# Which engine copies the attention output out of PSUM, and when in a head's turn

## The chip, the cores and the metric

The kernel runs on one core of one Trainium2 chip. The metric is the device time of one execution in microseconds (us). The kernel before was run three times: median 3234.82 us, lowest 3233.41, highest 3235.3.

## What is computed

A residual stream of 4 sequences of 1024 tokens with 128 channels goes through eight blocks: linear attention, a mixture of experts, full attention, the same mixture of experts, causal attention, a one-expert mixture, a row-sum attention, and the one-expert mixture again. Only the third block bears on the change. Cut to what matters:

```python
def _L0_attn_b_ref(hidden_states, Wq, bq, Wk, bk, Wv, bv, Wo, bo):   # 16 heads of 8
    q = (hidden_states @ Wq.T + bq).reshape(b, s, HEADS, HEAD_DIM) * SCALE
    k = (hidden_states @ Wk.T + bk).reshape(b, s, HEADS, HEAD_DIM)
    v = (hidden_states @ Wv.T + bv).reshape(b, s, HEADS, HEAD_DIM)
    scores = jnp.einsum('bqhd,bkhd->bhqk', q, k)
    probs = jax.nn.softmax(scores, axis=-1)
    out = jnp.einsum('bhqk,bkhd->bqhd', probs, v).reshape(b, s, d)
    return out @ Wo.T + bo
```

With 4 sequences and 16 heads there are 64 heads (the code's HEADS), each with 1024 queries and 1024 keys.

## The kernel before, in words

`full_attention` (L1956) first projects queries, keys and values (`project_qkv`) and writes them to DRAM, then runs `attend` (L1041), and last `attention_output` (L1727), which reads what `attend` stored. Each engine has its own program; programs are joined by counting semaphores, which the code wraps as "steps" (`o_read.wait(pe, n)` waits until step n of `o_read` is done). Every engine carries out its own instructions in order.

`attend` is written as turns: `run` (L1087) calls each engine's `step(i, n)` for n from 0 to 66. Turn n works on up to four heads at once. Head i = n has its **first pass**: for each of 8 query tiles, two matmuls (L1146 and L1147, `first_pass`) put 128 x 1024 scores into two PSUM banks, and VectorE takes the row maximum (L1253, `TENSOR_REDUCE`, eight in a turn, called maxima 0 to 7 here). There are two such bank pairs (banks 0 and 1, 2 and 3), used in turn, so tile m waits until maximum m - 2 is done (L1144). GpSimd splits the maxima into two bf16 halves (L1266, L1269), TensorE transposes them for head n - 1 in the second quarter of the turn (`turn_shift`, L1179), ScalarE copies them to SBUF (L1236) and SP writes them into the stacked queries by DMA (L1289).

Head j = n - 2 has its **second pass**: 16 score matmuls of 128 x 512 (`second_scores`, L1161) go through three PSUM banks (4 to 6, with one place in the rotation given to the transposed maxima), ScalarE takes the exponentials (L1226, 16 in a turn) into a ring of eight SBUF tiles, and TensorE weighs the values with them: `weigh` (L1171), four blocks of eight matmuls, all accumulated in bank 7 (`OB`). The last block of a head comes a turn late: it belongs to head n - 3.

TensorE's turn is four quarters g = 0 to 3. Each is: scores 4g, 4g+1, 4g+2; one block of weighted values (in quarter 0 the last block of head n - 3, in the others block g - 1 of head n - 2); score 4g+3; first-pass tiles 2g and 2g+1; in quarter 1 also the transpose.

The **output's bank** 7 holds head n - 3 until its last block is done in quarter 0. It must then be copied to SBUF before the first block of head n - 2, in quarter 1, may overwrite it: `weigh(j, 0)` waits for `o_read` (L1167). In the kernel before ScalarE makes this copy (`read_output`, L1213 to L1217, 128 x 512 f32 into one of two slots of `o_out`), after exponentials 0 to 3 of its turn and before exponential 4. It waits for the last weighted-value matmul of the head (L1214) and, from head 2 on, for the DMA that stored the same slot two heads before (L1216). SP waits for `o_read` and stores the slot to DRAM (L1284); on SP's queue this stands behind the seven loads of the next head (L1036, L1038, L1134).

VectorE's turn has nothing but the eight maxima. At maximum 0 it also waits until GpSimd has split the maxima of two heads ago (L1250). In the last turns, n = 64 to 66, there is no first pass and VectorE has nothing to do.

Of the kernel before, what the change touches and what calls it, by code (L numbers as in the profile page):

```python
# [8 lines left out]
ACT = mybir.ActivationFunctionType  # L9
# [1031 lines left out]
def attend(nc, S, space, vd):  # L1041

    ctx, sb, sem, steps = space
    ps = S.ps
# [3 lines left out]
    S1, S2, OB = 0, 4, 7  # L1048
# [3 lines left out]
    NT = len(tiles)  # L1052
# [16 lines left out]
    o_out = sb("o_out", [P, 2, GROUP])  # L1069
# [5 lines left out]
    stored = [sem(f"stored{n}") for n in range(2)]  # L1075
# [6 lines left out]
    def bank(n):  # L1082
        return S2 + place(n) % RING2
# [3 lines left out]
    def run(eng, step):  # L1087

        for c in range(HEADS + 3):
            step(Head(0, c), c)  # L1090

    def there(n, h):

        return n is None or 0 <= n - h < HEADS
# [7 lines left out]
    def attach(project):  # L1102
# [104 lines left out]
            run(pe, step)  # L1207

        def scalar(act):
            for s in (exped, m_read, o_read):  # L1210
                s.open(act)

            def read_output(h, n):  # L1213
                pv_mm.wait(act, h.times(NT, NT - 1))  # L1214
                if n is None or n - 3 >= 2:
                    act.wait_ge(stored[h.slot(2)], h.rounds(2) * 16)  # L1216
                nc.scalar.activation(o_out[:, h.slot(2), :], ps[:, OB, :], ACT.Copy).then_inc(o_read.sem, 1)  # L1217

            def step(i, n):
                j = i - 2  # L1220
                for g in range(4):
                    for m in range(4 * g, 4 * g + 4):
                        if there(n, 2):
                            s2_mm.wait(act, j.times(NT, m))
                            pv_mm.wait(act, j.times(NT, m - RING))
                            nc.scalar.activation(prob[:, m % RING, :], ps[:, bank(m), :],  # L1226
                                                 ACT.Exp).then_inc(exped.sem, 1)
                    if g == 0 and there(n, 3):
                        read_output(i - 3, n)
                    if g == 1 and there(n, 1):  # L1230
                        h = i - 1
                        m_mm.wait(act, h.times(1))
                        if n is None or n - 3 >= 0:

                            act.wait_ge(shifted[h.slot(2)], h.rounds(2) * 16)
                        nc.scalar.activation(shift_rows[0:SHIFT * KTS, h.slot(2), :],  # L1236
                                             ps[0:SHIFT * KTS, MAX_BANK, 0:P // 2].bitcast(BF16),
                                             ACT.Copy).then_inc(m_read.sem, 1)

            nc.scalar.activation(S.act_warm[:], S.eps[:], ACT.Exp)  # L1240
            run(act, step)

        def vector(dve):
            maxed.open(dve)

            def step(i, n):
                for m in range(KTS):
                    if there(n, 0):
                        if m == 0:
                            split.wait(dve, i.times(1, -2))  # L1250
                        s1_mm.wait(dve, i.times(KTS, m))
                        first = S1 + 2 * (m % 2)
                        nc.vector.tensor_reduce(neg_max[:, i.slot(2), m:m + 1],  # L1253
                                                ps[:, first:first + 2, :].rearrange("p b n -> p (b n)"),
                                                AX.X, ALU.max, negate=True).then_inc(maxed.sem, 1)

            run(dve, step)
# [52 lines left out]

        ahead.sync, ahead.gpsimd, ahead.clear = sync_ahead, gpsimd_ahead, clear_first
        return Programs(tensor, vector, scalar, gpsimd, sync)

    ahead = Shared()
# [1459 lines left out]
```

## Time and profile before

| | before |
|---|---|
| median of three runs | 3234.82 us |
| the profiled execution, its own time | 3234.58 us |
| its span, first to last instruction | 3232.9 us |
| instructions | 47502 |
| mean granted TensorE clock (share of 2.4 GHz) | 0.934 |
| `attend`, first matmul to last output copy | 336.9 to 1049.2 us |

In profile rows PE is TensorE's matmuls, PEld its weight loads (they may run beside and ahead of matmuls), DVE is VectorE, ACT ScalarE, POOL GpSimd, SPq the DMA queue that SP issues on. L1253 is line 1253 of the kernel. Times are us from the start of the span, unless ns is said. A row of a timeline may merge several like instructions that follow each other (x8); it gives their first start and the time to the last end. What stands in brackets is the idle time of the engine before the row, and what ended it; "issue" means that it waited for nothing the profile shows. PEclk is the granted clock as a share of 2.4 GHz.

### The profile page before, as it was taken

The page shows a single profiled execution, that of the slowest core. Times are in us where ns is not written, and L with a number is a line of the kernel's source. Part 1 is how long each engine was busy: PE and PEld are TensorE (multiplying, and loading weights), DVE is VectorE, ACT ScalarE, POOL GpSimd, SP SyncE. Part 2 cuts the span into 40 slices and gives each one's busy share as a digit, 9 for nine tenths or more (in the row PEclk, how much of TensorE's full clock was granted, in tenths as well). Part 3 has the DMA queues.
Part 4 walks back from the last instruction along what each step waited for, and adds up shares of the span by engine and source line. Part 5 has one row for each costly group of instructions (what it writes and reads, how often), then busy time and mean ns, then how long its engine had stood idle before and what let it go on. Part 6 is the DMA issues. An engine that isn't in the chain of part 4 may idle for free. (4 is left out here: it accounts for less than half of the span.)

```text
span 3232.9 us, 47502 instructions
## 1 busy us (share of the span) xinstructions
PE 2513.5 (78%) x12729; PEld 1044.9 (32%) x12911; DVE 2434.3 (75%) x4025; ACT 1832.9 (57%) x3590; POOL 1223.4 (38%) x1651
## 2 busy tenths in 40 slices
PE   5797799999999698799999999696745555555575
PEld 4543222222222443233333333284521010101454
DVE  6667788888886566777777777264279999999833
ACT  1212588888888111255555555303239999999521
POOL 1014533333331213378888888703550000000154
PEclk9899899999999699899999999887979999999688
DMA  3001322222221302712222222352131111110012
GB/s 94 1 1 62 100 79 71 78 71 78 71 79 54 95 1 77 252 61 80 81 83 77 73 80 68 107 211 60 40 109 40 33 32 32 33 33 26 18 45 81
DMA packets 192110, 223.46 MB, mean 69 GB/s; under 512 B 55152, under 2 KB 120944, under 8 KB 191472
## 3 DMA queue, kind: packets, MB, share of 16 engines
q1 hardware_dynamic: 152256, 192.41, 18.4%
q0 software_dynamic: 29696, 23.27, 3.1%
q10 hardware_dynamic: 9968, 5.51, 0.6%
q8 instruction: 87, 1.43, 0.2%
q14 instruction: 103, 0.84, 0.1%
HBM read 136.67 MB, written 83.76 MB: 68 GB/s over the span
## 5 line engine op out<-in xcount | busy, mean ns | idle before, releaser
L1253 DVE TENSOR_REDUCE neg_max<-ps 128x1 f32<-128x1024 f32 x512 | 602.5, 1219 | 93.8 <-PE ps L1147 87.0
L1632 POOL TENSOR_TENSOR acc<-acc,prob 128x512 f32<-128x512 f32 (+3 forms) x640 | 577.8, 943 | 87.5 <-PE ps L1481 87.5
L1226 ACT ACTIVATE prob<-ps 128x512 f32<-128x512 f32 x1024 | 556.3, 601 | 88.1 <-PE ps L1161 74.8
L2071 DVE TENSOR_REDUCE neg_max<-ps 128x1 f32<-128x1024 f32 x512 | 579.3, 1210 | 3.2 <-PE ps L2057 3.2
L2093 ACT ACTIVATE ps<-ps,neg_max 128x1024 f32<-128x1024 f32 x512 | 557.2, 1088 | 0.3 <-DVE neg_max L2071 0.3
L2057 PE MATMUL ps<-k_stack,q_stack 128*128 128x512 bf16 x992 | 303.5, 386 | 277.1 <-ACT ps L2093 273.9
L1561 ACT ACTIVATE prob<-ps 128x512 f32<-128x512 f32 (+3 forms) x640 | 266.5, 477 | 247.9 <-PE ps L1465 122.1
L1602 DVE TENSOR_REDUCE neg_max<-ps 128x1 f32<-128x128 f32 (+7 forms) x512 | 388.0, 758 | 17.5
L1161 PE MATMUL ps<-q_stack,k_stack 128*128 128x512 bf16 x946 | 292.8, 386 | 6.8 <-ACT prob L1226 4.6
L1171 PE MATMUL ps<-prob,v 128*32 128x512 f32 x2048 | 280.9, 620 | 3.7 <-ACT prob L1226 0.7
L1600 DVE TENSOR_TENSOR ps<-ps,mask_qk 128x128 f32<-128x128 f32 x512 | 151.1, 295 | 148.3 <-PE ps L1438 144.8
L1438 PE MATMUL ps<-k_stack,q_stack 72*128 72x512 bf16 (+3 forms) x768 | 217.1, 340 | 37.9 <-DVE neg_max L1602 26.6
L2193 POOL TENSOR_TENSOR x_res<-x_res,w_b_bo_row 128x512 f32 x8 | 12.6, 1613 | 583.5 <-SPq L2155 583.5
L583 PE MATMUL ps<-f_wd,hT 128*128 128x512 f32 x512 | 228.9, 601 | 0.0
L1481 PE MATMUL ps<-prob,v 128*64 128x512 f32 (+3 forms) x1280 | 228.0, 477 | 0.4 <-ACT prob L1561 0.4
L2057 PEld LDWEIGHTS ps<-k_stack,q_stack 128*128 128x128 bf16 x1024 | 58.7, 97 | 521.6 <-ACT ps L2093 516.9
L1465 PE MATMUL ps<-q_stack,k_stack 128*128 128x512 bf16 (+3 forms) x704 | 206.4, 327 | 20.9 <-ACT prob L1561 14.0
L1161 PEld LDWEIGHTS ps<-q_stack,k_stack 128*128 128x128 bf16 x1024 | 78.5, 97 | 315.6 <-ACT prob L1226 212.6
L1146 PE MATMUL ps<-k_stack,q_stack 64*128 64x512 bf16 x512 | 162.7, 391 | 21.8 <-DVE neg_max L1253 10.3
L1266 POOL TENSOR_TENSOR shift<-neg_max,zeros 128x8 bf16<-128x8 f32 x64 | 12.4, 195 | 432.3 <-DVE neg_max L1253 432.3
L1147 PE MATMUL ps<-k_low,q_low 64*128 64x512 bf16 x512 | 162.8, 391 | 0.0
L700 DVE SCALAR_TENSOR_TENSOR x_res<-ps,comb,x_res 128x128 f32<-128x128 f32 x256 | 88.2, 345 | 86.8 <-PE ps L583 86.6
(304 smaller groups left out, 3820.0 us busy)
## 6 DMA issues: line engine op xcount, KB each, us to landing
q_stack<-q_parts SPq DMA_DIRECT2D x576, 48.0 KB
k_stack<-k_parts SPq DMA_DIRECT2D x576, 48.0 KB
o_quads<-o_out SPq DMA_DIRECT2D x64, 256.0 KB
v<-v_wide SPq DMA_DIRECT2D x32, 512.0 KB
o_pairs<-o_out SPq DMA_DIRECT2D x64, 256.0 KB, 6.2
num<-o_pairs SPq DMA_DIRECT2D x8, 2048.0 KB
q_parts<-parts SPq DMA_DIRECT2D x24, 384.0 KB, 2.7
k_parts<-parts SPq DMA_DIRECT2D x24, 384.0 KB, 2.7
```

The source lines that it names most:

```text
L583: op = nc.tensor.matmul(ps[:, YB + 2 * (k % 2) + half, :], hT[:, g % 2, f, k * P:(k + 1) * P], S.f0_wd[:, f, half * GROUP:(half + 1) * GROUP],
L1161: nc.tensor.matmul(ps[:, bank(n), :], ks[j.slot(4)][:, kt * P:(kt + 1) * P], qs[j.slot(4)][:, c * GROUP:(c + 1) * GROUP], start=True, stop ...
L1171: nc.tensor.matmul(ps[quad:quad + VW, OB, :], vs[j.slot(4)][:, :, kt], prob[:, n % RING, :], start=kt < 2, stop=kt >= KTS - 2).then_inc(pv ...
L1226: nc.scalar.activation(prob[:, m % RING, :], ps[:, bank(m), :], ACT.Exp).then_inc(exped.sem, 1)
L1253: nc.vector.tensor_reduce(neg_max[:, i.slot(2), m:m + 1], ps[:, first:first + 2, :].rearrange("p b n -> p (b n)"), AX.X, ALU.max, negate=T ...
L1481: nc.tensor.matmul(ps[h * VD:(h + 1) * VD, OB + c, offset(u):GROUP], v, weights(j, u, h), start=kt == 0, stop=kt == (c + 1) * GROUP // P - ...
L1561: nc.scalar.activation(weights(j, u, h), ps[:, bank(2 * u + h), offset(u):GROUP], ACT.Exp).then_inc(exped.sem, 1)
L1602: nc.vector.tensor_reduce(neg_max[:, i.slot(2), m // KTS, qt:qt + 1], ps[:, bank:bank + c + 1, :].rearrange("p b n -> p (b n)") [:, 0:(qt ...
L1632: nc.gpsimd.tensor_tensor(sums, sums, weights(j, u, h), ALU.add).then_inc(added.sem, 1)
L2057: op = nc.tensor.matmul(ps[:, 2 * (qt % 4) + c, :], qs[i.slot(4)][:, qt * P:(qt + 1) * P], ks[i.slot(4)][:, c * GROUP:(c + 1) * GROUP], st ...
L2071: nc.vector.tensor_reduce(neg_max[:, i.slot(2), qt:qt + 1], ps[:, 2 * (qt % 4):2 * (qt % 4) + 2, :], AX.XY, ALU.max, negate=True).then_inc ...
L2093: nc.scalar.activation(s, s, ACT.Exp, bias=neg_max[:, i.slot(2), qt:qt + 1], accum_out=sums[:, cols(i.times(KTS, qt), 1)]).then_inc(summed ...
```

## The change

VectorE makes the copy of bank 7, as the first instruction of its turn, ahead of maximum 0; ScalarE no longer makes it. The waits go with the copy: on the last weighted-value matmul and on the store of the slot. `o_read` is counted by VectorE. Nothing else differs; SP and TensorE wait for `o_read` at the same places as before.

```diff
         def scalar(act):
-            for s in (exped, m_read, o_read):
+            for s in (exped, m_read):
                 s.open(act)
-
-            def read_output(h, n):
-                pv_mm.wait(act, h.times(NT, NT - 1))
-                if n is None or n - 3 >= 2:
-                    act.wait_ge(stored[h.slot(2)], h.rounds(2) * 16)
-                nc.scalar.activation(o_out[:, h.slot(2), :], ps[:, OB, :], ACT.Copy).then_inc(o_read.sem, 1)
...
-                    if g == 0 and there(n, 3):
-                        read_output(i - 3, n)
...
         def vector(dve):
             maxed.open(dve)
+            o_read.open(dve)
+
+            def read_output(h, n):
+                pv_mm.wait(dve, h.times(NT, NT - 1))
+                if n - 3 >= 2:
+                    dve.wait_ge(stored[h.slot(2)], h.rounds(2) * 16)
+                nc.vector.tensor_copy(o_out[:, h.slot(2), :], ps[:, OB, :]).then_inc(o_read.sem, 1)
 
             def step(i, n):
+                if there(n, 3):
+                    read_output(i - 3, n)
                 for m in range(KTS):
```

## Rows read from the trace of the kernel before

**Rows 1.** The page: each engine's busy time over the whole span.
```profile
PE 2513.5 (78%) x12729; PEld 1044.9 (32%) x12911; DVE 2434.3 (75%) x4025; ACT 1832.9 (57%) x3590; POOL 1223.4 (38%) x1651
```

**Rows 2.** Stretches: us; PE, PEld, DVE, ACT, POOL busy; PEclk, DMA share, GB/s.
```profile
400.00:1020.00 620.00, 608.66 (x3675) 165.62 (x3737) 542.26 (x462) 537.43 (x1037) 216.59 (x458) 1.00 0.25 74
2400.00:3000.00 600.00, 315.00 (x1048) 65.90 (x1080) 594.25 (x532) 589.65 (x1040) 20.39 (x19) 1.00 0.12 38
```

**Rows 3.** Line L1217, 400 to 1020 us: ns min/median/max, first and last start.
```profile
L1217 ACT ACTIVATE o_out<-ps x58: 592/592/592, 404.2 to 1018.4; 128x512 f32<-128x512 f32 x58
```

**Rows 4.** Lines, 400 to 1020 us: busy us, mean ns | idle before, releasers.
```profile
L1253 DVE TENSOR_REDUCE neg_max<-ps 128x1 f32<-128x1024 f32 x462 | 544.1, 1219 | 78.2 <-PE ps L1147 78.2
L1226 ACT ACTIVATE prob<-ps 128x512 f32<-128x512 f32 x922 | 501.3, 602 | 73.9 <-PE ps L1161 65.9
L1161 PE MATMUL ps<-q_stack,k_stack 128*128 128x512 bf16 x850 | 262.1, 384 | 3.7 <-ACT prob L1226 2.1 <-issue 1.0
...
L1217 ACT ACTIVATE o_out<-ps 128x512 f32<-128x512 f32 x58 | 34.3, 592 | 0.0
```

**Rows 5.** Who waited for whom, 400 to 1020 us: total us, times, longest us.
```profile
PEld ps L1171 <- ACT o_out L1217: 24.6, 58, 0.4
```

**Rows 6.** Timeline of one steady turn: start us, us, engine, line, shapes [idle before].
```profile
692.36 2.35 DVE L1253 TENSOR_REDUCE neg_max<-ps 128x1 f32<-128x1024 f32 x2 [0.28 <-PE ps L1147]
...
693.22 1.09 PE L1171 MATMUL ps<-prob,v 128*32 128x512 f32 x8
...
695.07 2.36 DVE L1253 TENSOR_REDUCE neg_max<-ps 128x1 f32<-128x1024 f32 x2 [0.36 <-PE ps L1147]
...
695.86 0.22 PEld L1171 LDWEIGHTS ps<-prob,v 128*32 128x32 f32 x8 [0.42 <-ACT o_out L1217]
...
696.99 0.47 SPq L1284 DMA_DIRECT2D o_quads<-o_out  x1
...
697.21 0.39 PE L1146 MATMUL ps<-k_stack,q_stack 64*128 64x512 bf16 x1
...
697.48 0.09 PEld L1146 LDWEIGHTS ps<-k_stack,q_stack 64*128 64x128 bf16 x1 [0.18 <-DVE neg_max L1253]
...
697.64 2.35 DVE L1253 TENSOR_REDUCE neg_max<-ps 128x1 f32<-128x1024 f32 x2 [0.21 <-PE ps L1147]
...
698.71 1.09 PE L1171 MATMUL ps<-prob,v 128*32 128x512 f32 x8
...
701.35 0.22 PEld L1171 LDWEIGHTS ps<-prob,v 128*32 128x32 f32 x8 [0.42 <-issue]
...
702.70 0.39 PE L1146 MATMUL ps<-k_stack,q_stack 64*128 64x512 bf16 x1
...
702.92 0.38 PE L1146 MATMUL ps<-k_stack,q_stack 64*128 64x512 bf16 x1
```

**Rows 7.** Groups by line, VectorE, whole span: copies from PSUM and a like operation.
```profile
L967 DVE TENSOR_TENSOR prob<-ps,w_a_bv_row 128x512 f32<-128x512 f32 x32 | 21.8, 689 | 5.3 <-PE ps L870 5.2
...
L679 DVE COPY totals<-ps 128x128 f32<-128x128 f32 x4 | 1.2, 292 | 0.8 <-PE ps L567 0.8
...
L502 DVE COPY totals<-ps 128x256 f32<-128x256 f32 x2 | 0.8, 424 | 1.4 <-PE ps L496 1.4
```

**Rows 8.** Timeline of a later stage: elementwise pieces following each other on VectorE.
```profile
1204.39 0.34 DVE L712 SCALAR_TENSOR_TENSOR other<-ps,comb,other 128x128 f32<-128x128 f32 x1
1204.65 0.34 DVE L700 SCALAR_TENSOR_TENSOR x_res<-ps,comb,x_res 128x128 f32<-128x128 f32 x1
```

**Rows 9.** Timeline after the last first pass: score matmuls and the blocks behind them.
```profile
1029.35 0.39 PE L1161 MATMUL ps<-q_stack,k_stack 128*128 128x512 bf16 x1 [0.26 <-ACT prob L1226]
...
1029.83 1.10 PE L1171 MATMUL ps<-prob,v 128*32 128x512 f32 x8
...
1034.59 0.39 PE L1161 MATMUL ps<-q_stack,k_stack 128*128 128x512 bf16 x1 [0.26 <-ACT prob L1226]
...
1034.91 1.10 PE L1171 MATMUL ps<-prob,v 128*32 128x512 f32 x8
```

## The prediction, made before the change was run

> **What bounds the kernel now.** I began with the engines' shares [rows 1]: TensorE is busy 78% of the 3232.9 us span and VectorE 75%, so a mean over all stages decides nothing. Only the attention stage of `full_attention` is touched. In its steady part, 400 to 1020 us, TensorE is busy 608.66 of 620 us at a granted clock of 1.00, its 2.4 GHz level; VectorE 542.26, ScalarE 537.43 [rows 2]. The output copy is one ScalarE instruction of 592 ns for each of the 64 heads, and in the steady part its 58 starts lie (1018.4 - 404.2)/57 = 10.775 us apart [rows 3]: that is a head's turn.
>
> The instructions by line over the same stretch show who has room [rows 4]. 620 us are 57.5 turns: per turn VectorE works 9.42 us, on eight maxima, and idles 1.35; ScalarE works 9.34 and idles 1.43, most of it until the next scores are there. Matmul instructions hardly wait at all. The waits list says otherwise at first sight: TensorE's weight loads wait 24.6 us for the output copy, once a turn [rows 5]. The loads may run ahead of the matmuls, so their waits need not be matmul time. The timeline of one turn decides that [rows 6]. The four blocks of eight weighted-value matmuls (L1171) start at 693.22, 695.86, 698.71 and 701.35: quarters of 2.64, 2.85 and 2.64 us, and 10.775 less these is 2.64 for the fourth. The load that waits 0.42 us for the output copy (695.86) belongs to a quarter exactly as long as the third, where the same 0.42 is "issue" (701.35). So TensorE's own sequence sets the pace, the output copy on ScalarE costs the turn nothing, and the longer quarter is the one that holds the transpose of the shift (L1179).
>
> But VectorE follows closely. The first maximum of the turn starts at 695.07, after 0.36 us of idleness that ends with first-pass matmul L1147. Two maxima take 2.36 us together. The first pass owns two bank pairs, so tile 3's matmuls wait until maximum 1 has emptied its pair. They do wait: their weight load starts at 697.48 behind "DVE neg_max", 0.27 us after tile 2's at 697.21, whereas the second pair elsewhere follows its first by 0.22 (702.70 to 702.92). So this one edge, maximum 1 to tile 3, is already late by 0.05 us per turn, and whatever delays maximum 0 delays TensorE.
>
> **The change, part by part.**
>
> *ScalarE loses the copy.* 0.59 us of its time per turn, with a wait on the weighted values and one on the store. Worth nothing in steady turns: exponential 4 may start about 0.1 us earlier, but the matmul block behind it was not held up (above), and ScalarE then waits for scores again.
>
> *VectorE gets the copy, ahead of maximum 0.* No 128x512 copy from PSUM is in this trace. The COPY rows take 292 ns for 128 columns and 424 for 256, so 1.03 ns a column and 688 ns for 512; a 128x512 tensor_tensor that reads PSUM takes 689 [rows 7]. I take 0.69. Lower end: the 256-column copy's 0.42. Upper end: 0.69 with nothing overlapped. Neighbours on VectorE do overlap: two maxima of 1.22 take 2.36 [rows 4, 6], and elementwise pieces of 0.34 that read PSUM start 0.26 apart [rows 8]. So an instruction starts 0.08 before its predecessor ends, and the copy occupies 0.61.
>
> *Its wait.* It waits for the last weighted-value block of head i-3, started at 693.22 and done at 694.31. The maxima before it (two from 692.36, 2.35 long) end at 694.71, so even for a start at 694.64 the block is ready 0.3 us early. Eight maxima are queued behind it, but the wait is met. The second wait, for the store of two heads ago, was met on ScalarE too (no idleness stands before L1217 [rows 4]).
>
> *The sum.* Copy from 694.64 to 695.33, maximum 0 from 695.25 in place of 695.07: 0.17 to 0.18 us late (0.61 less 0.08 overlap and 0.36 idleness). Maximum 1 ends as much later, tile 3's matmuls start as much later, and as this edge is already late, none is absorbed. What comes after TensorE runs in order, so the delay stays: maximum 2 waits for tile 2, which is not late (697.64 still holds). VectorE has its slack back, but TensorE has lost 0.17, and its instructions have no waits to make it up from [rows 4]. The next turn repeats it. It applies while a first pass runs beside an output, turns 3 to 63: 61 turns. 61 x 0.17 = 10.4 us.
>
> *The waits that go.* In the two turns after the last first pass, the value block starts 0.48 after its last score (1029.35 to 1029.83), against 0.32 elsewhere (1034.59 to 1034.91) [rows 9]: here ScalarE's copy does hold it. VectorE is idle then, so about 2 x 0.16 = 0.3 us return. The very last copy is alone on the path and becomes 0.1 longer. Together -0.2.
>
> *Other queues.* SP's store of the output waits for the copy, done at 695.33, but it is issued at 696.99 [rows 6], behind the seven loads of the next head on the same queue; no DMA moves. GpSimd's split of the maxima waits for maximum 7, which moves with TensorE. TensorE's wait for the emptied output bank is met 0.5 us before its block: no cost; if that cover were gone it would cost directly.
>
> Sum: +10.2 us on the profiled execution's 3234.58 us (span 3232.9) gives 3244.8; the median of the three runs, 3234.82, is 0.24 above it, so 3245.0.
>
> **A rule against the trace.** The two maxima in 2.36 us show that VectorE starts an instruction before its neighbour has ended [rows 6]. The Trainium skill, "VectorE: DVE Perf Modes", section "The DRAIN you can't avoid", says that the next operation doesn't start until the pipe is empty; this trace disagrees, by 0.08 us per pair, for reductions and elementwise pieces. Whether it holds between a copy and a reduction, no row of this stage shows. By that rule the sum would be the second rival's.
>
> **Rivals.**
> 1. *No change.* The copy hides: if it occupied no more than 0.44 us (the 0.36 idleness and the overlap), maximum 0 would start on time. The 256-column copy would (0.42 - 0.08 = 0.34); 512 columns at the rate of the rows would not. Or TensorE catches up by waits it now has; it has almost none [rows 4]. 3232 to 3237 us.
> 2. *Dearer.* The copy starts only when the maximum has ended (694.71), maximum 0 only when the copy has (695.40): 0.33 late, 61 x 0.33 = 20 us less the 0.2, 3255; with 0.1 us of start-up more, a guess since no row has a copy between two maxima, 3261.
> 3. *Faster.* If the 24.6 us that weight loads wait for the output copy [rows 5] were matmul time, the change would give it back, and 3210 would be the floor (3234.6 less 24.6). Its place is the block at 695.86, and it decides only if that quarter exceeds 2.64, which it doesn't. A gain also needs VectorE's addition to stay under the 0.44 us. More likely a remnant: 0.05 us per turn, 3 us, 3231.
> 4. *Clock.* TensorE with 1.6% more idleness could be granted 1.2 GHz for a while; it kept 1.00 through 600 us of a later stage where it was busy only half of the time [rows 2]. Some 5 to 10 us on top of the forecast.
>
> **How the numbers follow.** Forecast 0.74 (own range 3242 to 3248), no change 0.08, dearer 0.13, faster 0.03, clock 0.02. The range runs from 3239 (a copy that occupies 0.51 us: 61 x 0.07 less 0.2) to 3256, which takes in the first form of the dearer case; what is left out is below 0.2. A measurement of this kernel can tell about 0.2%, 6.5 us: slower is above 3241.3. Of the no-change mass and the low tail of the forecast I put 0.11 into "same"; 0.03 faster, 0.86 slower.
>
> **What would show it.** Right: L1217's successor on VectorE x64 at about 0.69 us, VectorE busy some 40 us more, ScalarE 38 less; maximum 0 without idleness before it; the copies' starts 10.95 us apart; the tile-3 load later by 0.17 relative to tile 2's (0.44 in place of 0.27); only the second quarter grown, to 3.02. Wrong: a turn still of 10.78; idleness before VectorE's copy (then the value block is the late one); other quarters grown; a granted clock below 1.00 between 400 and 1020 us (rival 4); growth outside this stage.

## The result and the profile after

The change takes 3244.09 us (median of 8 runs, 3240.08 to 3247.72) against 3233.71 us for the kernel before (8 runs, 3231.39 to 3235.93): the ratio is 1.0031, with a 95% interval of 1.0020 to 1.0042. It is slower by 10.4 us (3244.09 - 3233.71). The profiled execution took 3244.85 us, its span is 3242.9 us; 3245.0 us had been forecast. In two of the later series the kernel before itself took some 43 us longer (3278.03 and 3277.43 us), which in the traces of those series lies behind this stage, so a whole time is compared only with that of the kernel before in the same series.

The engines' busy time over the whole span, as in [rows 1]:

```profile
PE 2548.8 (79%) x12910; PEld 1044.8 (32%) x12911; DVE 2467.6 (76%) x4089; ACT 1807.8 (56%) x3526; POOL 1223.5 (38%) x1651
```

Then the busy times of the steady stretch (columns as in [rows 2]), and the line of VectorE's copy over the same stretch (columns as in [rows 3]).

```profile
400.00:1020.00 620.00, 617.93 (x3693) 163.38 (x3686) 563.78 (x513) 508.00 (x966) 216.15 (x456) 1.00 0.25 74
```

```profile
L1243 DVE COPY o_out<-ps x57: 680/681/683, 403.8 to 1015.7; 128x512 f32<-128x512 f32 x57
```

The same line over the whole span:

```profile
L1243 DVE COPY o_out<-ps x64: 680/681/692, 371.0 to 1057.2; 128x512 f32<-128x512 f32 x64
```

The granted clock is still 1.00, TensorE's 2.4 GHz level. The copies start (1015.7 - 403.8)/56 = 10.927 us apart, against 10.775 in [rows 3]: a turn has grown by 0.152 us. One copy takes 681 ns. TensorE's busy time has risen, 608.66 to 617.93 us, with no more work done: the trace of the kernel before lacks some matmul records (it has 12729 matmuls for 12911 weight loads, this one 12910), so the two busy times of TensorE can't be compared, and of the 11 us in which it seemed idle before the change a large part is probably missing records.

The groups by line show who gained and lost room (busy us, mean ns | idle before, as in [rows 4]), and the waits list what became of the 24.6 us of [rows 5]:

```profile
L1254 DVE TENSOR_REDUCE neg_max<-ps 128x1 f32<-128x1024 f32 x456 | 536.6, 1219 | 56.9 <-PE ps L1147 53.0
L1220 ACT ACTIVATE prob<-ps 128x512 f32<-128x512 f32 x909 | 493.6, 597 | 94.9 <-PE ps L1161 91.7
...
L1243 DVE COPY o_out<-ps 128x512 f32<-128x512 f32 x57 | 38.8, 681 | 0.0
```

```profile
PEld ps L1171 <- issue: 85.4, 227, 0.4
...
PEld ps L1146 <- DVE neg_max L1254: 31.3, 112, 0.5
```

VectorE's idleness before the maxima fell from 78.2 to 56.9 us, and none stands before its copy. ScalarE idles 94.9 us before its exponentials instead of 73.9. The weight loads of L1171 no longer wait for the output copy, and have as much idleness as before under another name: "issue" 85.4 us in 56.7 turns, where the kernel before had 62.0 of "issue" beside the 24.6 of [rows 5] in 57.5 turns, 1.51 us a turn both times. So that wait was none of TensorE's time. The timeline of one turn, to be laid beside [rows 6]:

```profile
685.76 2.36 DVE L1254 TENSOR_REDUCE neg_max<-ps 128x1 f32<-128x1024 f32 x2 [0.28 <-PE ps L1147]
...
686.62 1.10 PE L1171 MATMUL ps<-prob,v 128*32 128x512 f32 x8
...
688.03 0.68 DVE L1243 COPY o_out<-ps 128x512 f32<-128x512 f32 x1
...
688.63 4.77 DVE L1254 TENSOR_REDUCE neg_max<-ps 128x1 f32<-128x1024 f32 x4
...
689.26 1.10 PE L1171 MATMUL ps<-prob,v 128*32 128x512 f32 x8
...
690.39 0.53 SPq L1285 DMA_DIRECT2D o_quads<-o_out  x1
690.60 0.09 PEld L1146 LDWEIGHTS ps<-k_stack,q_stack 64*128 64x128 bf16 x1 [0.23 <-issue]
...
691.02 0.09 PEld L1146 LDWEIGHTS ps<-k_stack,q_stack 64*128 64x128 bf16 x1 [0.33 <-DVE neg_max L1254]
...
692.25 1.10 PE L1171 MATMUL ps<-prob,v 128*32 128x512 f32 x8
...
694.04 2.36 DVE L1254 TENSOR_REDUCE neg_max<-ps 128x1 f32<-128x1024 f32 x2 [0.64 <-PE ps L1147]
...
694.90 1.10 PE L1171 MATMUL ps<-prob,v 128*32 128x512 f32 x8
...
697.54 1.10 PE L1171 MATMUL ps<-prob,v 128*32 128x512 f32 x8
```

Maximum 0 follows the copy with no gap (688.03 to 688.63), and four maxima run on end for 4.77 us. Tile 3's weight load starts 691.02 - 690.60 = 0.42 us after tile 2's, behind "DVE neg_max"; it was 0.27. The blocks of weighted values stand at 686.62, 689.26, 692.25, 694.90 and 697.54: quarters of 2.64, 2.99, 2.65 and 2.64 us. Only the second has grown, from 2.85; the first, at whose end the output copy was waited for, is as long as it was. By maximum 4 (694.04) VectorE is idle 0.64 us again.

The last copy of the stage starts at 1057.2 us, 8.6 later than ScalarE's last one did (1048.6), and that in a stage that began 0.3 earlier (first maximum at 339.0 us, not 339.3): 8.9 us, against 61 turns (3 to 63) of 0.152 = 9.3, less 0.3 that the stage's end gives back (see below). The other 1.3 us by which the span grew lie behind the stage, where the two programs don't differ: from the end of the last copy on it took 2183.7 us before and 2185.0 after, and in the traces of the other kernels, the two slower series aside, 2182.7 to 2185.1.

### The profile page after: what moved, and what is told of

Same layout as the page of the kernel before. It is cut to its first block and busy times, and to the rows that moved or that the text cites. A ratio compares the mean times of both kernels' runs of the same rounds, so it can differ in the third digit from the quotient of the medians.

```text
span 3242.9 us, 47683 instructions
## 1 busy us (share of the span) xinstructions
PE 2548.8 (79%) x12910; PEld 1044.8 (32%) x12911; DVE 2467.6 (76%) x4089; ACT 1807.8 (56%) x3526; POOL 1223.5 (38%) x1651
## 5 line engine op out<-in xcount | busy, mean ns | idle before, releaser
L2058 PE MATMUL ps<-k_stack,q_stack 128*128 128x512 bf16 x1024 | 311.9, 387 | 268.3 <-ACT ps L2094 265.0
L1161 PE MATMUL ps<-q_stack,k_stack 128*128 128x512 bf16 x1024 | 311.6, 386 | 2.2 <-ACT prob L1220 2.2
L1171 PE MATMUL ps<-prob,v 128*32 128x512 f32 x2048 | 280.8, 620 | 0.7 <-ACT prob L1220 0.7
L1466 PE MATMUL ps<-q_stack,k_stack 128*128 128x512 bf16 (+3 forms) x768 | 224.3, 332 | 21.2 <-ACT prob L1562 14.4
L1146 PE MATMUL ps<-k_stack,q_stack 64*128 64x512 bf16 x512 | 169.6, 391 | 18.7 <-DVE neg_max L1254 9.5
L1147 PE MATMUL ps<-k_low,q_low 64*128 64x512 bf16 x512 | 169.6, 391 | 0.0
```

The source lines that it names most:

```text
L1161: nc.tensor.matmul(ps[:, bank(n), :], ks[j.slot(4)][:, kt * P:(kt + 1) * P], qs[j.slot(4)][:, c * GROUP:(c + 1) * GROUP], start=True, stop ...
L1171: nc.tensor.matmul(ps[quad:quad + VW, OB, :], vs[j.slot(4)][:, :, kt], prob[:, n % RING, :], start=kt < 2, stop=kt >= KTS - 2).then_inc(pv ...
L2058: op = nc.tensor.matmul(ps[:, 2 * (qt % 4) + c, :], qs[i.slot(4)][:, qt * P:(qt + 1) * P], ks[i.slot(4)][:, c * GROUP:(c + 1) * GROUP], st ...
```

## The experiments

The theory tested, A: the copy fills VectorE's gap ahead of maximum 0 and overruns it; this delays maximum 1, and this alone delays first-pass tile 3 on TensorE. The rivals: B, that VectorE stands in its queue behind a wait on TensorE; C, that ScalarE's relief is worth something; D, that every column on VectorE costs, without a threshold. The turn is read in every experiment from the first and last start of the output's copy between 400 and 1020 us, divided by the count less one. Such a mean holds a few turns that are longer by some tenths of a us. The change has one: there maximum 0 starts 0.81 us after the copy, and not 0.60, and the profile shows nothing that it waits for:

```profile
676.89 0.68 DVE L1243 COPY o_out<-ps 128x512 f32<-128x512 f32 x1
...
677.70 4.62 DVE L1254 TENSOR_REDUCE neg_max<-ps 128x1 f32<-128x1024 f32 x4
```

So where thousandths matter the median distance from one maximum 0 to the next is given too: 10.773 us before, 10.923 with the change. What makes single turns longer is open.

**How long may the copy be?** Three kernels cut it, all with this edit (n = 1, 256, 384) and with the output tile filled with ones once, ahead of the first turn:

```diff
-                nc.vector.tensor_copy(o_out[:, h.slot(2), :], ps[:, OB, :]).then_inc(o_read.sem, 1)
+                nc.vector.tensor_copy(o_out[:, h.slot(2), 0:n], ps[:, OB, 0:n]).then_inc(o_read.sem, 1)
```

One column:

> The change with VectorE's copy cut to one column; the other 511 columns of the stored output are a constant, so later stages work on other values. Theory A (the copy's length delays maximum 0, hence maximum 1, hence first-pass tile 3 on TensorE): a one-column copy occupies under 0.1 us, less than the 0.44 us that VectorE has there, so the steady turn is 10.775 us as before the change, tile 3's weight load 0.27 us after tile 2's, time 3232 to 3236 us. Rival B (not the length costs, but that VectorE stands in the queue behind a wait on TensorE's last block): 10.92 as with the change. Rival C (ScalarE's relief is worth the 0.42 us per turn that weight loads waited for it): 10.35 to 10.7.

256 columns:

> The change with VectorE's copy cut to 256 of 512 columns, the rest of the stored output a constant. A: the copy takes 0.42 us and occupies 0.33 to 0.34, under the 0.44 us of slack, so the turn is 10.775 us. B: 10.92. A cost in proportion to the columns, without a threshold (rival D), would give 10.85.

384 columns:

> The change with VectorE's copy cut to 384 of 512 columns, the rest of the stored output a constant. A: 384 columns occupy 0.598 - 128 x 0.00104 = 0.465 us; with the change the slack proved to be 0.598 - 0.152 = 0.446; so 0.02 us are lost in a turn: 10.795 us. D (in proportion): 10.89. B: 10.92.

The copy's row of each, in this order (ns min/median/max, first and last start):

```profile
L1246 DVE COPY o_out<-ps x58: 147/149/149, 401.8 to 1016.1; 128x1 f32<-128x1 f32 x58
```

```profile
L1246 DVE COPY o_out<-ps x58: 414/415/416, 402.0 to 1016.2; 128x256 f32<-128x256 f32 x58
```

```profile
L1246 DVE COPY o_out<-ps x58: 548/548/550, 404.5 to 1019.9; 128x384 f32<-128x384 f32 x58
```

The turns are 614.3/57 = 10.777, 614.2/57 = 10.775 and 615.4/57 = 10.796 us; the times of one run each are 3233.49, 3233.16 and 3236.09 us, with 3234.99 for the kernel before on the same chip. A put them at 10.775, 10.775 and 10.795. B falls: the one-column copy waits for the same block of TensorE and stands at the same place, and it costs nothing. D falls too: half of the columns cost nothing, the next quarter 0.02 us, the last quarter 0.13, which is what its 128 columns take on VectorE (681 - 548 ns). C falls: in these kernels ScalarE is relieved and VectorE not burdened, and the turn is that of the kernel before to 2 ns.

**VectorE's work alone.** ScalarE keeps the copy; VectorE gets an instruction that waits for nothing, into a new tile of four slots:

```diff
             def step(i, n):
+                if there(n, 3):
+                    nc.vector.tensor_tensor(spare[:, i.slot(4), :], S.x[:, 0:GROUP], S.x[:, GROUP:2 * GROUP], ALU.add)
                 for m in range(KTS):
```

> The kernel before, ScalarE keeping its copy, with one VectorE instruction added ahead of maximum 0: a 128x512 addition of two pieces of the residual stream into a spare tile, about 0.68 us, waiting for nothing. A: the addition alone does what the change does: 10.92 to 10.93 us, time about 3243 us. B: no wait on TensorE, so 10.775. C (the change lost more on VectorE than it shows and got part back from ScalarE): well over 10.93.

```profile
L1218 ACT ACTIVATE o_out<-ps x57: 592/592/592, 403.5 to 1015.6; 128x512 f32<-128x512 f32 x57
```

(1015.6 - 403.5)/56 = 10.930 us, and 3241.82 us against 3234.99 (single runs differ by 6.8; 61 turns of 0.155 make 9.5, and the stage itself is 9.2 us longer). The turn of the change comes back, within 0.003 us, though neither the copy nor its waits have moved. So the whole of the cost is VectorE time ahead of maximum 0, for any instruction of that length. And as ScalarE's copy is still there, this says once more that removing it was worth nothing in a steady turn.

**Twice as much.** The same addition, put behind the copy in the change:

```diff
                 if there(n, 3):
                     read_output(i - 3, n)
+                    nc.vector.tensor_tensor(spare[:, i.slot(4), :], S.x[:, 0:GROUP], S.x[:, GROUP:2 * GROUP], ALU.add)
                 for m in range(KTS):
```

> The change, with a further VectorE instruction between the copy and maximum 0: a 128x512 addition of two pieces of the residual stream into a spare tile that nobody reads. A: past the threshold each us on VectorE costs a us of the turn: 10.926 + 0.60 = 11.53 us, time about 3281 us. If TensorE could make the delay up in later quarters (rival), less.

The copy's row, and the timeline at tile 3:

```profile
L1244 DVE COPY o_out<-ps x54: 678/680/681, 407.2 to 1017.9; 128x512 f32<-128x512 f32 x54
```

```profile
695.29 0.68 DVE L1244 COPY o_out<-ps 128x512 f32<-128x512 f32 x1
...
695.89 0.68 DVE L1249 TENSOR_TENSOR spare<-x_res 128x512 f32<-128x512 f32 x1
...
696.49 3.48 DVE L1256 TENSOR_REDUCE neg_max<-ps 128x1 f32<-128x1024 f32 x3
...
697.87 0.39 PE L1147 MATMUL ps<-k_stack,q_stack 64*128 64x512 bf16 x1
...
698.89 0.39 PE L1147 MATMUL ps<-k_stack,q_stack 64*128 64x512 bf16 x1 [0.63 <-DVE neg_max L1256]
```

(1017.9 - 407.2)/53 = 11.523 us: 0.596 more than with the change, and the addition starts 0.60 us before maximum 0 does (695.89 to 696.49). Past the threshold the turn pays for VectorE one to one; TensorE now visibly stands 0.63 us before tile 3. The whole time is 3319.97 us, against 3278.03 for the kernel before in this series: 41.9 more. 61 turns of 0.748 make 45.6, and the stage, from first maximum to last copy, is 45.4 us longer, so single runs carry such a sum to within a few us only, and the turn is the better measure.

**Moving tile 3.** If the edge from maximum 1 to tile 3 is all, the copy must be free once TensorE has something to do between tiles 2 and 3. The transpose of the shift, which followed tile 3, is put there, with the copy on VectorE (first) and on ScalarE (second):

```diff
                     if one:
                         first_pass(i, 2 * g)
-                        first_pass(i, 2 * g + 1)
                     if g == 1 and there(n, 1):
                         turn_shift(i - 1, j if two else None)
+                    if one:
+                        first_pass(i, 2 * g + 1)
```

> The change, with TensorE's transpose of the shift moved from behind first-pass tile 3 to between tiles 2 and 3. A: tile 3 stands 0.475 us behind tile 2 in TensorE's own sequence (0.32 to the transpose, 0.155 from it), more than the 0.42 at which maximum 1 releases it, so the copy on VectorE is hidden: turn 10.81 us (the split pair costs 0.04 over the kernel before), 0.11 less than with the change. B or any cost elsewhere in the turn: stays at 10.92 or more.

> The kernel before with the same move of the transpose between tiles 2 and 3, the copy staying on ScalarE. A: 10.81 us, the same as with the copy on VectorE. If the copy's cost lies on another edge, the two differ by about 0.15 as the kernels before and after do.

```profile
L1244 DVE COPY o_out<-ps x58: 678/680/682, 402.1 to 1019.3; 128x512 f32<-128x512 f32 x58
```

```profile
L1218 ACT ACTIVATE o_out<-ps x57: 592/592/592, 403.4 to 1009.5; 128x512 f32<-128x512 f32 x57
```

617.2/57 = 10.828 and 606.1/56 = 10.823 us. The copy's engine makes 0.005 us of difference where it made 0.152, and the median turn is 10.823 us in both. Both lose 0.05 to the kernel before, 0.01 to 0.02 more than expected; the likely reason is that the pair of tiles is torn apart, which no run shows by itself. Single runs took 3278.04 and 3279.47 us (3278.03 for the kernel before); they are too few to rank them.

**A better place for the transpose.** Ahead of score 7 it comes before both tiles and keeps them together. Again with the copy on VectorE (first) and on ScalarE (second):

```diff
                         weigh(i - 3, 3)
+                    if g == 1 and there(n, 1):
+                        turn_shift(i - 1, j if two else None)
                     if two:
                         second_scores(j, 4 * g + 3, there(n, 1))
...
-                    if g == 1 and there(n, 1):
-                        turn_shift(i - 1, j if two else None)
```

> The change, with TensorE's transpose moved ahead of score 7, so that tiles 2 and 3 come 0.155 us later in its sequence. A: tile 3 would be released 0.27 us behind tile 2, nearly the 0.227 of an unhindered pair: turn 10.77 us, time 3234 us. If moving it costs a switch elsewhere: up to 10.86.

> The kernel before with the same transpose ahead of score 7. A: the 0.05 us that tile 3 waits in the kernel before go: turn 10.725 us, 3 us less, 3230 to 3232 us, the fastest of all. If this wait was not real: 10.775.

```profile
L1243 DVE COPY o_out<-ps x58: 678/679/682, 404.7 to 1018.7; 128x512 f32<-128x512 f32 x58
```

```profile
696.59 1.57 ACT L1220 ACTIVATE prob<-ps 128x512 f32<-128x512 f32 x3 [0.26 <-PE ps L1161]
...
696.91 1.09 PE L1171 MATMUL ps<-prob,v 128*32 128x512 f32 x8
...
697.83 0.22 PE L1179 MATMUL ps<-ident_b,shift 128*16 128x128 bf16 x1
...
698.30 0.09 PEld L1146 LDWEIGHTS ps<-k_stack,q_stack 64*128 64x128 bf16 x1 [0.23 <-issue]
...
698.68 0.09 PEld L1146 LDWEIGHTS ps<-k_stack,q_stack 64*128 64x128 bf16 x1 [0.29 <-DVE neg_max L1254]
```

```profile
L1217 ACT ACTIVATE o_out<-ps x58: 591/591/591, 402.4 to 1013.2; 128x512 f32<-128x512 f32 x58
```

```profile
692.38 1.58 ACT L1226 ACTIVATE prob<-ps 128x512 f32<-128x512 f32 x3
...
692.59 1.10 PE L1171 MATMUL ps<-prob,v 128*32 128x512 f32 x8
...
693.62 0.22 PE L1179 MATMUL ps<-ident_b,shift 128*16 128x128 bf16 x1
...
694.09 0.39 PE L1146 MATMUL ps<-k_stack,q_stack 64*128 64x512 bf16 x1
...
694.31 0.38 PE L1146 MATMUL ps<-k_stack,q_stack 64*128 64x512 bf16 x1
```

With the copy on VectorE the turn is 614.0/57 = 10.772 us and the time 3234.68 us (11 runs; the kernel before 3234.58 in 21), a ratio of 1.0001 to the kernel before (0.9992 to 1.0010): the loss of the change is made good. With the copy on ScalarE the turn is 610.8/57 = 10.716 us, tile 3 follows tile 2 by the unhindered 0.22, and the time is 3230.54 us (11 runs), ratio 0.9988 (0.9979 to 0.9997): 4 us faster than the kernel before and the fastest complete kernel of all.

The turns came out as forecast (median turns 10.767 and 10.710 us), but not by the parts forecast. With VectorE's copy the tile-3 load still waits for the maximum, 0.38 us behind tile 2's and not 0.27: the transpose (697.83, 0.92 us behind its block) delays tile 2 by only 0.04, not 0.155. That changed nothing in the sum, as it is maximum 1 and not tile 2 that releases tile 3: tile 3's load stands 1.77 us behind its block (698.68 - 696.91), as with the change (691.02 - 689.26 = 1.76), and the gain is that the transpose no longer follows it. With ScalarE's copy the transpose starts 1.03 us behind its block (693.62 - 692.59), and the exponentials of that quarter 0.21 ahead of it (692.38) in place of 0.32 (696.59 to 696.91). The transpose waits for exponential 5 (L1178), so here, for the first time, ScalarE's copy seemed to cost something. A further kernel asked that, with both edits, this order and the one-column copy:

> The change with the transpose ahead of score 7 and VectorE's copy cut to one column; the other 511 columns of the stored output are a constant, so later stages work on other values. The two kernels with the early transpose left a question: the transpose came 0.92 us behind its block with VectorE's copy and 1.03 with ScalarE's. Theory E: in this order the transpose waits for exponential 5, which ScalarE reaches 0.11 us sooner without its copy, so here its relief is worth 0.1 us, while VectorE's 512-column copy costs 0.16 at tile 3. With neither on the path tile 2 comes as with VectorE's copy, tile 3 0.227 behind it, and the turn is 10.772 - 0.155 = 10.61 to 10.62 us. Rival F (the 0.11 us comes from something else in the order, such as VectorE's work): 10.71 to 10.72, as with ScalarE's copy.

```profile
L1246 DVE COPY o_out<-ps x58: 146/149/158, 403.6 to 1009.8; 128x1 f32<-128x1 f32 x58
```

(1009.8 - 403.6)/57 = 10.635 us; a single run took 3262.5 us where the kernel before took 3277.43, and the stage is 9.5 us shorter than in the kernel before. E holds, F falls: with neither copy in the way the order gives 0.08 us less than with ScalarE's copy and 0.14 less than with VectorE's. In this order ScalarE's relief is worth about 0.1 us a turn, and VectorE's burden costs more than that. The median turn is 10.620 us, as forecast; five turns that are longer by up to 0.31 us, as single ones are in other kernels, make the mean 0.02 more.

**One place later.** The copy between maxima 0 and 1:

```diff
-                if there(n, 3):
-                    read_output(i - 3, n)
                 for m in range(KTS):
+                    if m == 1 and there(n, 3):
+                        read_output(i - 3, n)
```

> The change with VectorE's copy one place later, between maximum 0 and maximum 1. A: tile 3's edge would cost the same, but now the other end of the copy's room decides: it ends 2.31 us after tile 0's matmul starts (maximum 0 at 0.50, the copy 1.13 later, 0.68 long), while the first block of the next head would start 1.29 after it. TensorE's block waits about 1.05 us, the first-pass tiles come as much later and no longer wait for maxima: turn 10.725 + 1.05 to 1.1 = 11.8 us, time about 3297 us. Rival (only VectorE's total work counts, 10.0 us per turn, not where the copy stands): 10.93.

```profile
L1243 DVE COPY o_out<-ps x52: 680/681/683, 408.5 to 1010.6; 128x512 f32<-128x512 f32 x52
```

```profile
PE ps L1171 <- DVE o_out L1243: 53.0, 52, 1.0
```

(1010.6 - 408.5)/51 = 11.806 us, 3298.53 us against 3233.77. VectorE's work is that of the change; now TensorE's matmuls wait 53.0/52 = 1.02 us in each turn for the output's bank. So it isn't VectorE's total that counts: the copy has a room between maximum 7 and its bank's next block, and it overran the room's other end here.

## Why the prediction was right

It was right in size, sign and mechanism. By its own steps:

- *What bounds.* TensorE's sequence, with the edge from maximum 1 to tile 3 already late. Shown by the quarters of the turn after and by both moves of the transpose. The 0.05 us of tile 3 fit the kernel with the early transpose and ScalarE's copy, 0.06 us shorter, but no run isolates them.
- *ScalarE's relief is worth nothing in this order.* Shown by the one-column copy (10.777 us) and from the other side by VectorE's addition alone.
- *The copy's cost.* 0.69 us was read from shorter copies; it measured 0.681. Its occupation, 0.61 forecast, is 0.60 (688.03 to 688.63), and the threshold of 0.44 is bracketed: 256 columns fit, 384 are 0.02 us over. The term came out at 0.152 us instead of 0.17, so 9.3 us for the 61 turns instead of 10.4. The difference is two hundredths: the copy is 0.01 us shorter, and it starts 0.09 us before the maximum ahead of it ends (685.76 + 2.36 = 688.12, the copy at 688.03), not 0.08.
- *Its waits.* No idleness stands before the copy in the steady stretch: the last block was done in time, as forecast, and so was the store. *Other queues:* SP issues the store of the output 1.13 us behind the start of its bank's next block, before (696.99 - 695.86) and after (690.39 - 689.26), so it did not move.
- *The end of the stage.* In the first turn after the last first pass the trace has the value block 0.32 us behind its score, as forecast, where it was 0.48 [rows 9]:

```profile
1038.27 0.39 PE L1161 MATMUL ps<-q_stack,k_stack 128*128 128x512 bf16 x1 [0.26 <-ACT prob L1220]
...
1038.59 1.10 PE L1171 MATMUL ps<-prob,v 128*32 128x512 f32 x8
```

  The same holds one turn later (1048.41 to 1048.73; before, 1039.66 to 1040.15). From the end of the last maximum to the end of the last copy it took 1028.74 to 1049.17 = 20.43 us before and 1037.66 to 1057.85 = 20.19 after: 0.24 us gained, with 0.2 forecast. The last copy's start alone comes 0.34 earlier in this count; the copy, 0.09 longer, takes that part back.
- *The signs named.* Copies 10.927 us apart (10.95 named), tile 3's load 0.42 behind tile 2's (0.44), the second quarter 2.99 (3.02). Two were off: VectorE is busy 33.3 us more over the span, not 40, and ScalarE 25.1 less, not 38. Both had counted whole instructions, but busy time counts overlapping neighbours once: 64 copies of 0.681 us, less 0.17 by which each overlaps the maxima on its two sides, are 32.7. TensorE's idleness, which the clock's rival put at 1.6% more, can't be read from the busy times (above). Growth outside the stage was named as a sign of being wrong; the 1.3 us found are no more than the scatter there.
- *The rivals.* No change would have needed a copy of at most 0.44 us; the 256-column kernel is that case. The dearer case needed neighbours that don't overlap. The Trainium skill, "VectorE: DVE Perf Modes", section "The DRAIN you can't avoid", has the next operation wait for an empty pipe, but goes on to say that a next operation that is not held starts earlier. The prediction left that exception out. Here a 681 ns copy is followed by a maximum after 0.60 us, 0.08 before the copy has ended, so between a copy and a reduction, too, the trace bears out the exception and not the bare rule. The granted clock stayed at 1.00 in the steady stretch.

The median's 10.4 us agree with the forecast's 10.2 better than its parts do, and that closeness is luck: 9.3 us of turns less the end's 0.24 are 9.0, and the remaining 1.4 us no trace ascribes to the change. The interval of the ratio, 1.0020 to 1.0042, is 6.5 to 13.6 us and holds both 9.0 and 10.4, so the 1.4 need no cause of their own, and none was found.

## What to carry to other kernels

A weight load that waits need not cost matmul time (here 0.42 us in each turn cost nothing): compare the length of the stretches with and without the wait before booking a gain. An engine that is busy 87% of a stretch may still have one spot where less than half a us is all the room there is; look for the consumer that already waits there (here 0.27 us between two loads where 0.22 is free), since whatever is put ahead of it beyond the free room is paid one to one, once per turn. Such a spot can be eased from the consumer's side: with one transpose moved ahead of it the copy on VectorE cost nothing net any more. But the order and the engine have to be chosen together; in the new order it was ScalarE's time that had a price.

## What the runs showed beyond that

VectorE's addition of two SBUF tiles, alone in the kernel before, made GpSimd's first piece of the split beside it take 571 ns instead of 194 (first row; the second is from the kernel with copy and addition):

```profile
L1269 POOL TENSOR_TENSOR shift<-neg_max,zeros 128x8 bf16<-128x8 f32 x57 | 32.5, 571 | 370.6 <-DVE neg_max L1256 370.6
```

```profile
L1269 POOL TENSOR_TENSOR shift<-neg_max,zeros 128x8 bf16<-128x8 f32 x54 | 10.6, 196 | 403.2 <-DVE neg_max L1256 403.2
```

In the kernel with copy and addition that same piece runs beside the copy out of PSUM instead, and takes 196 ns. So a copy from PSUM left GpSimd alone where an addition of two SBUF operands slowed it nearly threefold. In one turn the addition runs from 698.18 to 698.86 and the piece from 698.35 to 698.92, ending 0.06 us behind it. It cost no time here (the turn is that of the change to 0.003 us), but it could where GpSimd is on the path; no run tried an addition with one operand in PSUM.
